# Perceiver block on one core: who loads the attention's keys, in what pieces, and behind what

## What is computed

```python
x = x + _L0_xattn_ref(_layernorm(x), ctx_512, Wq, w_kc_q, w_kc_kv, W_qr, W_kr, Wo)   # x: 2 x 256 x 512
x = x + _L0_attn_ref(_layernorm(x), Wq, Wk, Wv, Wo)
x = x + _L0_ffn_ref(_layernorm(x), wq_gate, s_gate, wq_up, s_up, wq_down, s_down)

# in _L0_xattn_ref, 16 heads, keys kv_c: 2 x 4096 x 128
q_hk  = (hidden_q @ Wq.T).reshape(B, S, 16, 128)
q_big = apply_rope(einsum('bshk,hkq->bshq', q_hk, w_kc_q), sin_q, cos_q)      # width 384
kv_r  = apply_rope(kv_c, sin_k, cos_k)                                       # the keys' rotation
q_r   = einsum('bshq,hqr->bhsr', q_big, W_qr);  k_r = einsum('bld,hdr->bhlr', kv_r, W_kr)
attn  = softmax(einsum('bhsr,bhlr->bhsl', q_r, k_r))
ctx_c = einsum('bhsl,bld->bhsd', attn, kv_r)                                 # then w_kc_kv and Wo
```

## Time and profile before

| what | value |
|---|---|
| median of 3 runs | 1070.21 us (1066.58 to 1074.66) |
| the profiled execution's own time | 1078.67 us |
| its span, first to last instruction | 1076.9 us |
| TensorE matmul, weight load busy | 96%, 67% |
| VectorE, ScalarE, GpSimd busy | 80%, 70%, 58% |
| DMA moved | 180.15 MB, mean 167 GB/s |
| mean granted TensorE clock | 0.986 |

### The profile page before, as it was taken

One profiled execution on the slowest core, in us unless ns is written; L12 is line 12 of the kernel. 1 busy time (PEld: TensorE's weight loads), 2 busy tenths in 40 slices (PEclk: granted clock), 3 DMA queues, 4 the chain that ended last, 5 costly groups with the idle time before them and its releaser, 6 DMA issues.

```text
span 1076.9 us, 24647 instructions
## 1 busy us (share of the span) xinstructions
PE 1031.6 (96%) x9456; PEld 724.3 (67%) x9456; DVE 863.0 (80%) x1241; ACT 759.1 (70%) x1188; POOL 622.9 (58%) x812
## 2 busy tenths in 40 slices
PE   6789998999999999999999999999999999999988
PEld 4344544766766677777777777777777745768877
DVE  5799887989999999999998999999999604544633
ACT  2133338888888899989998999999999631426532
POOL 1983352788888877768777777777776412000000
PEclk9899999999999999999999999999999999998999
DMA  9443365999999999999999999999999960050000
GB/s 366 131 157 107 105 141 100 195 196 205 205 203 199 211 205 202 203 199 207 205 203 193 195 211 204 199 207 197 196 202 194 219 253 5 1 203 23 1 21 20
DMA packets 568933, 180.15 MB, mean 167 GB/s; under 512 B 551536, under 2 KB 557680, under 8 KB 568176
## 3 DMA queue, kind: packets, MB, share of 16 engines
q1 hardware_dynamic: 567456, 173.86, 76.9%
q10 hardware_dynamic: 1360, 4.72, 1.1%
HBM read 39.07 MB, written 1.05 MB: 37 GB/s over the span
## 4 chain that ended last, share of the span: by engine, by line
PE 83%; DMA 8%; DVE 5%; ACT 2%; issue 1%; POOLq 1%; SPq 0%; POOL 0%; ACTq 0%; DVEq 0%
PE ps_o L1316 10%; PE ps_o L1317 10%; PE ps_o L1320 10%; PE ps_s L1297 6%; PE ps_s L1299 6%; PE ps_s L1298 6%; DMA pt_both<-p_both 5%; PE ps_o L1377 5%; PE ps_t L1297 3%; PE ps_t L1298 3%; PE ps_t L1299 3%; PE ps_t L1217 2%; DMA kvr<-ctx_kv_dram 2%; PE ps_s L1194 1%; DVE wq_lo L875 1%; PE ps_s L1467 1%
## 5 line engine op out<-in xcount | busy, mean ns | idle before, releaser
L989 DVE SCALAR_TENSOR_TENSOR p_both<-prob,p_both 128x1024 f16<-128x1024 f32 x256 | 325.9, 1273 | 38.0 <-ACT p_both L674 33.1
L682 ACT ACTIVATE prob<-sized,nmax 128x1024 f32<-128x1024 f32 x256 | 293.3, 1146 | 28.7 <-DVE sized L1000 25.8
L674 ACT ACTIVATE p_both<-prob 128x1024 f16<-128x1024 f32 x256 | 270.6, 1057 | 34.3 <-DMA pt_both<-p_both 12.2
L1316 PE MATMUL ps_o<-kn,pt_both 128*128 128x128 f16 x2048 | 258.2, 220 | 11.2 <-DMA pt_both<-p_both 10.9
L1317 PE MATMUL ps_o<-kn,pt_both 128*128 128x128 f16 x2048 | 258.2, 220 | 0.0
L1316 PEld LDWEIGHTS ps_o<-kn,pt_both 128*128 128x128 f16 x2048 | 200.9, 98 | 47.8 <-DMA pt_both<-p_both 11.7
L1000 DVE TENSOR_SCALAR_CACHE_REDUCE sized<-ps_s,against 128x1024 f32<-128x1024 f32 x170 | 217.2, 1278 | 9.4 <-PE ps_s L1299 3.9
L1317 PEld LDWEIGHTS ps_o<-kn,pt_both 128*128 128x128 f16 x2048 | 201.4, 98 | 27.1
L1320 PE MATMUL ps_o<-kn,pt_both 128*128 128x128 f16 x2048 | 157.0, 220 | 0.0
L544 POOL TENSOR_TENSOR oscl<-ocopy,weigh 128x512 f32<-128x512 f32 x64 | 94.7, 1480 | 85.2 <-ACT ocopy L696 82.4
L1297 PE MATMUL ps_s<-kt,q_hi 128*128 128x512 f16 x340 | 128.9, 379 | 1.3 <-DVE qcos L907 1.3
(11 more groups left out here) (214 smaller groups left out, 1786.0 us busy)
## 6 DMA issues: line engine op xcount, KB each, us to landing
wgu_raw<-w_gu_dram SPq DMA_DIRECT2D x11, 512.0 KB, 9.9
wq_s<-wq_t_dram SPq DMA_DIRECT2D x16, 256.0 KB, 3.8
wot_s<-wo_t_dram SPq DMA_DIRECT2D x16, 256.0 KB, 2.8
kvr<-ctx_kv_dram ACTq DMA_DIRECT2D x4, 1024.0 KB, 12.7
pt_both<-p_both SPq DMA_TRANSPOSE x256, 4.0
kvr<-w_mix_dram SPq DMA_DIRECT2D x4, 1024.0 KB, 9.2
wkcq_s<-w_kcq_dram SPq DMA_DIRECT2D x16, 192.0 KB, 2.5
wdn_raw<-w_dn_dram SPq DMA_DIRECT2D x1, 2816.0 KB, 8.9
```

The source lines that it names most:

```text
L674: nc.scalar.mul(p_hi(n), prob[:, n % 2, :], PSCALE).then_inc(hi_done, 1)
L682: nc.scalar.activation(prob[:, n % 2, :], sized[:, n % 2, :], ACT.Exp, bias=nmax[:, i, c:c + 1], scale=-1.0, accum_out=rsum[:, i, c:c + 1] ...
L989: nc.vector.scalar_tensor_tensor(out=p_lo(n), in0=prob[:, n % 2, :], scalar=PSCALE, in1=p_hi(n), op0=ALU.mult, op1=ALU.subtract).then_inc( ...
L1316: nc.tensor.matmul(o, pt_hi[:, k, :], kn[:, b, p, 0, keys], start=(k == 0), stop=False)
```

## The change

ScalarE no longer loads keys, and `kv_in` is gone. `load_turn(p, i)` on SyncE issues a third transfer behind the two tables: the keys of piece p, 512 columns of both batches, 512 KB in rows of 2 KB, on the same semaphore; GpSimd waits for 48 per round in place of 32, and no longer for all the keys. The load of piece 1 and `load_rotated(1)` move from before the first `refill` into it, behind the weights of head 2 and before the wait for `b_done`. Pieces 2 to 7 come, as their tables did, behind the wait for `krope`.

```diff
@@ -196,7 +196,6 @@
-        kv_in = [sem(f"kv_in{i}") for i in range(4)]
@@ -352,6 +351,8 @@
                 for m, src in ((0, cos_k), (1, sin_k)):
                     sp.dma_start(cs_k[:, i, m, :], src[:, bass.ds(p * PIECE, PIECE)]).then_inc(cs_in[i], 16)
+                cols = slice(p * PIECE, (p + 1) * PIECE)
+                sp.dma_start(kvr[:, :, cols], kv_v[:, :, cols]).then_inc(cs_in[i], 16)
@@ -370,13 +371,14 @@
             load_rotated(0)
-            load_turn(1, 1)
-            load_rotated(1)
 
             def refill(h, i):
                 sp.wait_ge(a_done, h + 1)
                 load_wq(h + 2, i)
+                if h == 0:
+                    load_turn(1, 1)
+                    load_rotated(1)
                 sp.wait_ge(b_done, QC * (h + 1))
@@ -471,7 +473,7 @@
             def kv_rope(p, i, k):
-                pool.wait_ge(cs_in[i], 32 * k)
+                pool.wait_ge(cs_in[i], 48 * k)
@@ -488,9 +490,6 @@
             with pool.Fori(0, NP // 2) as pair:
-
-                for q in range(4):
-                    pool.wait_ge(kv_in[q], 16)
                 kv_rope(2 * pair, 0, pair + 1)
@@ -588,11 +587,7 @@
             nc.scalar.copy(mask[:, :], ps_o[:, 0, 0:P]).then_inc(mask_ok, 1)
-            act.wait_ge(x_in[0], 16)
-            act.wait_ge(x_in[1], 16)
-            for q in range(4):
-                cols = slice(q * L // 4, (q + 1) * L // 4)
-                act.dma_start(kvr[:, :, cols], kv_v[:, :, cols]).then_inc(kv_in[q], 16)
+
             def round_wq(i, k):
```

## The result

The changed kernel takes 1067.06 us in the median of 20 executions (1060.91 to 1070.14) beside 1071.35 for the kernel before (1064.57 to 1078.48, 20 executions): ratio 0.9955, 95% interval 0.9934 to 0.9977. Timed once more, it gave 0.9965 (0.9937 to 0.9992). So it is faster, by 0.4%, some 4 us. (The ratios are those of the record, and can lie some tenths of a per cent off the quotient of two medians, which is 0.9960 here.) Its profiled execution took 1069.38 us, 9.3 less than that of before. The profile moved by twice what the medians did; the second half of this text is about that.

The account below looks back on a forecast made before the run. Bound: TensorE, 96% busy, standing where head 3's weights wait behind SyncE's krope wait and wq_lo meets GpSimd. Gains 0.3 + 5.0 + 2.3 + 5.4 = 13.0, less 5.2 of collisions, 7.8 us: 1062.4, range 1056 to 1070.

Parts of the forecast that it names:

- Piece 0: First key piece, on SyncE's queue: lands at about 12.8 us, GpSimd rotates it until 20.9; worth 0.
- SyncE's order: Weights of head 3 leave SyncE at 24.2 in place of 33.71, so head 3 starts 5.0 us earlier without a collision.
- The stall and the clock: TensorE at heads 2 and 3: 5.0 us from head 3's earlier start, 2.3 from full clock, 0.3 from head 2.
- the 0.3 of head 2: TensorE's head 2 starts earlier, its weights no longer sharing the DMA with 4 MB of keys: 0.3 us gained.
- That of head 1: VectorE's wq_lo of head 1 meets GpSimd's rotation of the first piece, ending up to 2.2 us later: worth 0.
- Keys off ScalarE's queue: Four issues leave ScalarE, but TensorE's first head also needs the norm of x: worth 0, at most 2.21 us.
- Collisions: VectorE's wq_lo of heads 3 to 8 waits for GpSimd's rotation: 5.2 us by chance, 5.1 followed once.
- The keys' landing: Each 512 KB key load beside the heads: 0.9 us of issue and 5 of landing fit in GpSimd's 8.1; costs 0.
- Rival D: Late pieces starve GpSimd and hold up kmax: costs from a landing of 12.7 us, 1074.6 at 16.75; chance 0.03.
- I take the same difference off the median: Gain worked out on the profiled 1078.67 us, taken whole off the timed median: 1070.2 - 7.8 = 1062.4.

Follow-up runs that it names:

- weights_first: Kernel before, keys still in four 1 MB transfers on ScalarE; SyncE issues query weights of head h + 2 ahead of the wait for a piece's rotation: 1060.72 us, ratio 0.9905.
- no_rotation: Changed kernel without the keys' rotation: GpSimd's four operations of a piece touch one element each, all waits and loads stay: 1059.81 us, ratio 0.9899 to before.
- halved_ops: Changed kernel with GpSimd's two long operations of a piece each cut in two by batch: 1064.04 us, ratio 0.9933 to before.
- order_only: Kernel before with only SyncE's order changed: tables of piece 1 and rotated weights of pair 1 behind head 2's weights, keys still on ScalarE: 1072.09 us, ratio 1.0001.
- act_pieces: Kernel before with the keys still on ScalarE's queue, but in eight 512 KB pieces, GpSimd waiting for its piece alone: 1074.04 us, ratio 1.0011.
- early_second: Changed kernel with tables and keys of piece 1 and rotated weights of pair 1 issued ahead of the first refill again: 1064.28 us, ratio 0.9929 to before.

## Why the prediction was right, and where its size was off

*Direction, mechanism and range* held: 1067.06 lies in 1056 to 1070, and within 1%. *Piece 0, SyncE's order*: landed at 13.5 (12.8), weights of head 3 at 25.0 (24.2), both as worked out; weights_first shows that this wait was the cause.

*The stall and the clock.* Forecast 5.0 + 2.3 + 0.3. Head 3 started 3.9 us earlier and ran 2.3 shorter; the 0.3 of head 2 was a loss of 0.85 (28.95 against 28.10). Its weights did come early enough, but its `wq_lo` met GpSimd and waited 0.95, a meeting that I had missed. That of head 1 I had priced at 0, and it cost 0: TensorE began head 1 at 21.62, without a gap behind the wide products of head 0. *Keys off ScalarE's queue* I had priced at 0 to 2.21 us of gain, and it cost a little: ScalarE, free earlier, rounds the weights of head 0 at 6.58 in place of 8.19, so `wq_lo` of head 0 starts at 8.46, now ahead of GpSimd's root for the norm, and the root takes 0.36 us longer. GpSimd's timeline, before and after:

```profile
8.61 1.03 POOL L458 TENSOR_TENSOR rstd<-mv,mhalf 128x4 f32<-128x4 f32 x1 [6.23 <-DVE mv L871]
```

```profile
8.64 1.39 POOL L460 TENSOR_TENSOR rstd<-mv,mhalf 128x4 f32<-128x4 f32 x1 [6.26 <-DVE mv L866]
```

The norm follows 0.4 us later, and head 0 with it (14.72 against 14.33). All six profiles with the keys on SyncE's queue have the 1.39 or 1.40. Of the eight others seven have 1.03; the first of weights_first, in which `wq_lo` was also 0.07 us ahead of the root, has 1.50.

*Collisions.* Forecast 5.1 for heads 3 to 8; the profile shows 4.0 for these and 1.0 for head 2, and 4.7 in all the second time. The sum to the first score matmul, 8.2 us, stands beside 7.8 forecast. That they lie so near is in part luck: head 2 lost 1.1 us against the forecast, and the meetings of heads 3 to 8 gave 1.1 of it back. As a model for one execution the sum held; no_rotation and halved_ops confirm the part of the meetings from both sides.

*The keys' landing.* 5.6 to 7.5 us, where I took 5. GpSimd waited 3.8 us for pieces 4 to 7 and the last was rotated at 85.4, but `kmax` of it was wanted only at 97.73: cost 0, as forecast. Rival D did not come. The DMA moved 181 GB/s beside the heads, 149 before. Pieces 1 to 7 landed 6.6 to 8.2 us after the issue of their first table (piece 5 let GpSimd start 60.36 - 52.80 = 7.6 us after it), where I had counted 5.9. The transfers overlapped less than I assumed.

*The size of the median, and luck.* The step that failed is the first one: "I take the same difference off the median". About 8 us off the profiled execution is right, and 4.3 is what the medians gave, just inside the forecast's lower end of 4. Before's profiled execution lies 7.3 us above its median, the changed kernel's only 2.3 above its own; the tails of the two are alike, so what sets before's apart is above all its stage over heads, which I take for the upper kind of meetings. At the same mean clock (0.989, 0.992, 0.994) the changed kernel lies 6 to 8 us below the upper kind and about level with the lower one, at most 1.3 below it. Its 1078.67, above all three timed runs, was a sign of this that I named and did not use: the waits of `wq_lo` in it, two whole operations out of six, I priced as certain for before and as chance for after. Priced as chance on both sides, 5.2 against 5.2, the collisions give nothing, and the sum is the stall alone, by the working above 3.5 to 5.4 us: near the measured 4. That working was made after the result, and no run tested it by itself.

## What to carry to other kernels

SyncE, which issues the loads here, was a line: the weights of head 3 left at 33.71 behind its wait and at 24.86 ahead of it. So before moving data to another queue, look what stands behind each wait in the issuing program. Moving one wait gained at least as much (0.9905, 0.9934) as moving 4 MB (0.9955, 0.9965), and more in the one direct comparison (1061.58 against 1067.52). And where two engines meet in every round, one profile shows one pattern of meetings (two kernels of one median had their first score matmul at 162.0 and 154.5 here); price the meetings as chance on both sides, and hold the profiled time against several timed executions before a difference of profiles is taken for one of medians.

## What the runs showed of the hardware that was not expected

- VectorE's subtraction `wq_lo` (two SBUF tiles) and GpSimd's operations of the keys' rotation waited for one another: in before GpSimd was first (38.29 against 38.67), and `wq_lo` took 2.50 in place of 0.69 and ended at 41.17, 0.54 us after GpSimd's operation (40.63). In order_only `wq_lo` started 0.01 us earlier (38.05 against 38.06) and took 0.69, and GpSimd's operation was longer by about that (2.92 in place of 2.34). Not every meeting costs: in before GpSimd's root ran from 8.61 to 9.64 and `wq_lo` of head 0, begun at 8.84, took its 0.69. Between order_only's profile and before's, which part at the meeting at 38 us, lie 7.5 us in the first score matmul: 5.6 of waits and 1.9 of stall.
- VectorE's norm (`tensor_scalar`, one SBUF input, 128x512 fp32) was longer too, in act_pieces 8.01 us for four (13.41 to 21.42, beside GpSimd's rotation from 13.47 to 21.13) in place of 1.91; the maximum over the keys (`tensor_reduce`) was not: 1.21 us in all eight rounds of both kernels, in the changed one also at 35.29, beside GpSimd's products from 34.29 to 36.78.
- The granted clock fell after work had begun again: in order_only TensorE had stood 3.33 us, started at 38.79 at 1.00, and was at 0.50 from about 39.4. In early_second it had stood 2.38 us (its `wq_lo` of head 5 took 2.67), started at 55.01 and was at 0.50 from about 55.6. In before, with 5.52 us of standing, it fell while TensorE stood: 1.00 in 39.2 to 39.4 us, 0.56 in 39.4 to 39.6, 0.50 from there. After the changed kernel's 0.83 us and the 1.67 of weights_first's head 2 it stayed at 1.00.
- The tail took about 211.5, 214 or 217.4 us in executions of the same code, with a granted clock over the tail of 0.99, 0.98 or 0.96.
